# Selective scan in a vision tower: the input term made by TensorE from diagonals of B, decays in SBUF, the product with C split between GpSimd and VectorE

## What is computed

```python
xz = x_in @ W_in
x, z = (xz[..., :D], xz[..., D:])
proj = x @ W_x
B_ssm = proj[..., D:D + N]
C_ssm = proj[..., D + N:]
delta = jax.nn.softplus(delta_raw @ W_dt + b_dt)
A = -jnp.exp(A_log)
dA = jnp.exp(jnp.einsum('bld,dn->bldn', delta, A))
dBx = jnp.einsum('bld,bln->bldn', delta * x, B_ssm)
...
h = dA_t * h + dBx_t
y_t = jnp.einsum('bdn,bn->bd', h, C_t)
...
y = jnp.moveaxis(ys, 0, 1) + x * D_param
y = y * jax.nn.silu(z) @ W_out
```

## Time and profile before

| what | value |
| --- | --- |
| median of three runs | 780.34 us (776.89, 780.5, 780.34) |
| the profiled execution, its own time | 776.23 us |
| its span in the trace | 774.4 us |
| busy: PE, DVE, ACT, POOL | 689.5, 357.3, 255.4, 133.1 us |
| the first scan begins, the gated product begins | 203.87, 269.41 us |
| TensorE's mean granted clock | 0.989 |

### The profile page before, as it was taken

The page is one execution under the profiler, slowest core; times in us unless marked ns, Lnnn a source line. Parts: engine busy times, 40 slices in busy tenths (PEclk is TensorE's granted clock), DMA queues, the critical chain, the costliest instruction groups (busy, mean ns, idle before and its releaser), DMA issues.

```text
span 774.4 us, 16067 instructions
## 1 busy us (share of the span) xinstructions
PE 689.5 (89%) x6493; PEld 522.8 (68%) x6493; DVE 357.3 (46%) x1060; ACT 255.4 (33%) x639; POOL 133.1 (17%) x100
## 2 busy tenths in 40 slices
PE   9988879988866798989988989999977998999996
PEld 6665668875433356765754679888955556998985
DVE  3328640006999775667668641111136761111113
ACT  1332335543533414653691222222210122222221
POOL 2000200011399700131050220000040040000004
PEclk9999999999999999999999999999997999999999
DMA  8950179915566130000002789999228046899903
GB/s 310 405 217 0 36 240 422 375 62 197 156 150 149 36 123 1 0 1 0 1 0 83 306 279 353 348 378 348 98 64 349 1 176 214 345 357 363 363 29 92
DMA packets 30932, 143.85 MB, mean 186 GB/s; under 512 B 4624, under 2 KB 16720, under 8 KB 24336
## 3 DMA queue, kind: packets, MB, share of 16 engines
q1 hardware_dynamic: 23888, 132.86, 46.6%
q0 software_dynamic: 2240, 5.90, 2.4%
q10 hardware_dynamic: 4736, 4.13, 1.6%
HBM read 133.15 MB, written 9.71 MB: 184 GB/s over the span
## 4 chain that ended last, share of the span: by engine, by line
PE 55%; DVE 17%; issue 11%; DMA 6%; POOL 5%; ACT 3%; SPq 1%; DVEq 0%; POOLq 0%; ACTq 0%
PE PS L556 52%; DVE arena L2037 5%; POOL arena L1519 2%; DMA arena<-w_moe 2%; PE PS L615 1%; DMA x_slots<-XH,posu 1%; DMA arena<-y_slots,posu 1%; PE PS L579 1%; DVE stats L1600 1%; DVE stats L1593 1%; POOL arena L1545 1%; DMA arena<-bc_scratch 1%; DVE arena L2162 1%; DMA y_slots<-arena 1%; POOL arena L1532 1%
## 5 line engine op out<-in xcount | busy, mean ns | idle before, releaser
L556 PE MATMUL PS<-arena 128*64 128x64 f32 (+4 forms) x3132 | 243.9, 264 | 13.9 <-issue 5.2
L556 PEld LDWEIGHTS PS<-arena 128*64 128x64 f32 (+1 forms) x3132 | 203.8, 153 | 46.5 <-issue 20.8
L1823 DVE TENSOR_TENSOR arena<-arena,PS 128x384 f32<-128x384 f32 (+1 forms) x66 | 26.9, 407 | 183.4 <-ACT arena L1201 183.4
L556 PE MATMUL PS<-warm 128*128 128x512 bf16 (+2 forms) x425 | 97.5, 364 | 14.9 <-DVE rs L1584 13.5
L1519 POOL DMA_INDIRECT arena<-y_slots,posu x25 | 23.6, 945 | 312.2 <-DMA y_slots<-arena 305.5
L556 PEld LDWEIGHTS PS<-warm 128*128 128x128 bf16 (+1 forms) x425 | 38.7, 101 | 56.4 <-DVE rs L1584 16.8
L1201 ACT ACTIVATE arena<-PS 128x384 f32<-128x384 f32 (+1 forms) x66 | 27.2, 413 | 137.5 <-PE PS L556 137.5
L1532 POOL TENSOR_TENSOR arena<-arena 128x1152 f32<-128x1152 f32 x16 | 56.3, 3521 | 33.6 <-DVE arena L2037 33.6
L556 PE MATMUL PS<-arena,ident 128*128 128x512 f32 (+1 forms) x128 | 38.0, 440 | 21.5 <-POOL arena L1532 21.5
L556 PE MATMUL PS<-arena,wsh 128*128 128x128 f32 (+3 forms) x612 | 54.8, 260 | 1.3 <-ACT arena L1193 0.7
L556 PEld LDWEIGHTS PS<-arena,wsh 128*128 128x128 f32 (+1 forms) x612 | 48.6, 167 | 5.8 <-issue 2.8
(11 more groups left out here) (304 smaller groups left out, 929.7 us busy)
## 6 DMA issues: line engine op xcount, KB each, us to landing
arena<-w_moe SPq DMA_DIRECT2D x24, 2176.0 KB, 9.3
arena<-w_moe SPq DMA_DIRECT2D x9, 2052.0 KB, 10.8
wsh<-w_moe SPq DMA_DIRECT2D x8, 2176.0 KB, 9.9
arena<-bc_scratch SPq DMA_DIRECT2D x32, 288.0 KB, 3.9
wsh<-w_moe SPq DMA_DIRECT2D x3, 2052.0 KB, 12.0
y_slots<-arena ACTq DMA_DIRECT2D x19, 128.0 KB, 9.3
wx<-w_moe SPq DMA_DIRECT2D x1, 2176.0 KB, 17.6
wx<-w_sh SPq DMA_DIRECT2D x1, 2176.0 KB, 8.6
```

The lines of the kernel that those rows point to most:

```text
L556: return nc.tensor.matmul(out_, l, r, start=start, stop=stop, skip_group_check=True)
L1823: ins = v.tensor_tensor(firsts(hid_b[x][:, 0:full], n_), firsts(sg_s[x][:, 0:full], n_), firsts(PS[:, 2 * x + 1, 0:full], n_), ALU.mult)
```

## The change

TensorE now makes dBx. For each state and each tile of 128 tokens (the fifth has 64) ScalarE writes a diagonal matrix with the B values of that state's tokens (`state_diagonal`: the identity, scaled per partition by `BT`), and TensorE multiplies the transposed dx (`dxT`, tokens on partitions) with it: the product is dx with each token scaled, channels on partitions again, in PSUM (`XB`, one buffer per half). For that, TensorE computes B with tokens on partitions (ten products of 16 columns), and transposes dx (ten transposes, copied to SBUF by VectorE). The decays go to SBUF, two buffers per half (`dA`). VectorE's wide product is gone; the product with C is split along the tokens: GpSimd takes the first 480 of 576, VectorE the last 96, and in the last state 160 and 416. The loads of B rows are gone, and C rows are loaded once TensorE has read `hC` (hc_read). `keep_warm(3)` is removed.

```diff
-            return (PS[:, 0:2] if m else PS[:, 2:4])[:, :, 0:TH]
-        dA = [PS[:, 3 + 2 * d:5 + 2 * d, :].rearrange("p b c -> p (b c)")[:, 0:T] for d in range(KD)]
+            return (PS[:, 0:2] if m % 2 else PS[:, 2:4])[:, :, 0:TH]
+        XB = [PS[:, 4 + 2 * d:6 + 2 * d, :].rearrange("p b c -> p (b c)")[:, 0:T] for d in range(KD)]
-        dBx = part(8 * U1, 2, KD, T)
+        dA = part(8 * U1, 2, KD, T)
-        bcB = part(14 * U1, 4, T)
+        diagB = part(14 * U1, 2, NT, 128)
+        BT = part(14 * U1 + 2 * NT * 128, NT, NS)
+        C_CUT, C_CUT_LAST = 480, 160
...
-                    sp.wait_ge(sem("dbx_done"), 4 * i + (n - 3))
-                    sp.dma_start(bcB[:, n], bc_scratch[bass.ds(4 * i + n, 1), :].to_broadcast([128, T]))\
-                        .then_inc(sem(f"B{n}"), 16)
-                    sp.wait_ge(sem("hc_done"), 4 * i + (n - 1))
+                    sp.wait_ge(sem("hc_read"), 4 * i + (n - 1))
...
-                    pe.wait_ge(sem("xz_read"), m)
+                    pe.wait_ge(sem("xz_read"), m - 1)
                 from_xt([XZ_PS(m)[:, h, :] for h in range(2)], lambda k: win_s[:, k, 128 * m:128 * (m + 1)], "xz_psum")
+                if m == 1:
...
+                    for j in range(NT):
+                        for k in range(KD):
+                            last = mm(PS[:, 4, NS * j:NS * (j + 1)], XT[:, k, TT * j:TT * (j + 1)], wx_s[:, k, D:D + NS],
+                                      k == 0, k == KD - 1)
...
+            pe.wait_ge(sem("dx_ready"), 2)
+            for j in range(NT):
+                for d in range(KD):
+                    at = D * (j % 2) + 128 * d
+                    last = nc.tensor.transpose(PS[0:TILE_N[j], 5 + j // 2, at:at + 128], dx[:, d, tsl(j)], ident[:, :])
...
+            def state_input(n, d, p):
+                pe.wait_ge(sem("scan_half"), 2 * n + (d + 1))
+                for j in range(NT):
+                    last = mm(XB[d][:, tsl(j)], dxT[j][0:TILE_N[j], 128 * d:128 * (d + 1)], diagB[0:TILE_N[j], p, j, 0:TILE_N[j]])
+                last.then_inc(sem("xb"), 1)
+            def state_output(n, p):
+                pe.wait_ge(sem("hc_done"), n + 3)
+                pe.wait_ge(sem("hc_dve"), n + 1)
+                for d, ts, acc in Y_PARTS:
+                    last = mm(acc, ident[:, :], hC[:, p, d, ts], False, False)
+                last.then_inc(sem("hc_read"), 1)
...
-            keep_warm(3)
...
+            with pe.Fori(0, NS // 2 - 1) as i:
+                for p in range(2):
+                    pe.wait_ge(sem("diag_b"), 2 * i + (p + 4))
+                    for d in range(KD):
+                        state_input(2 * i + (p + 2), d, p)
+                    state_output(2 * i + p, p)
...
+                    last = nc.scalar.activation(diagB[0:n_, p, j, 0:n_], ident[0:n_, 0:n_], ACT.Copy, scale=BT[0:n_, j, bass.ds(n, 1)])
...
+                    act.wait_ge(sem("xb"), 4 * i + (2 * p + 2))
+                    state_diagonal(2 * i + (p + 2), p)
+                    for d in range(KD):
+                        act.wait_ge(sem("scan_half"), 4 * i + (2 * p + d + 3))
+                        decay(2 * i + (p + 2), d, p)
...
+                nc.gpsimd.tensor_tensor(hC[:, n % 2, :, 0:to], hs_[:, n % 2, :, 0:to],
+                                        bcC[:, n:n + 1, 0:to].to_broadcast([128, KD, to]), ALU.mult)\
+                    .then_inc(sem("hc_done"), 1)
...
-                v.tensor_tensor(dBx[:, n % 2, :, :], dx[:, :, :], bcB[:, n:n + 1, :].to_broadcast([128, KD, T]), ALU.mult)\
-                    .then_inc(sem("dbx_done"), 1)
...
+                    dve.wait_ge(sem("xb"), 8 * i + (2 * n + d + 1))
-                    v.tensor_tensor_scan(hs_[:, n % 2, d], dA[d], dBx[:, n % 2, d], 0.0, ALU.mult, ALU.add)\
+                    v.tensor_tensor_scan(hs_[:, n % 2, d], dA[:, n % 2, d], XB[d], 0.0, ALU.mult, ALU.add)\
...
+            def weigh(i, n, at):
+                dve.wait_ge(sem("scan_half"), 8 * i + (2 * n + 4))
+                dve.wait_ge(sem("hc_read"), 4 * i + (n + 1))
+                dve.wait_ge(sem(f"C{n}"), 16 * i + 16)
```

More of the change, by code:

```diff
@@ L938, in _ @@
             pe.sem_inc(sem("hc_read"), 2)
-            keep_warm(3)
[L940 to L945, removed]
+            state_input(1, 1, 1)
+            with pe.Fori(0, NS // 2 - 1) as i:
[4 more added lines that the diff above has]
+                    state_output(2 * i + p, p)
+            for p in range(2):
+                state_output(NS - 2 + p, p)
             idle_products(7)
@@ L1338, in _ @@
                 act.wait_ge(sem("dt_u"), m + 1)
-                nc.scalar.activation(dBx[:, 1, m], dBx[:, 0, m], ACT.Ln).then_inc(sem("dt_ln"), 1)
+                nc.scalar.activation(dA[:, 1, m], dA[:, 0, m], ACT.Ln).then_inc(sem("dt_ln"), 1)
                 xz_copy(m)
-            act.wait_ge(sem("A_ready"), 1)
[L1342 to L1350, removed]
@@ L1352, in _, with state_diagonal @@
-            decays(0)
+            act.wait_ge(sem("dxt_psum"), 1)
+            nc.scalar.activation(BT[:, :, :], PS[:, 4, 0:NT * NS].rearrange("p (j n) -> p j n", n=NS), ACT.Copy)\
+                .then_inc(sem("diag_b"), 1)
+            act.wait_ge(sem("diag_b"), 1)
+            def state_diagonal(n, p):
+                for j in range(NT):
+                    n_ = TILE_N[j]
+                    last = nc.scalar.activation(diagB[0:n_, p, j, 0:n_], ident[0:n_, 0:n_], ACT.Copy, scale=BT[0:n_, j, bass.ds(n, 1)])
+                last.then_inc(sem("diag_b"), 1)
@@ L1353, in _, with decay @@
+            def decay(n, d, p):
+                nc.scalar.activation(inner(dA[:, p, d]), inner(dl[:, d, :]), ACT.Exp, scale=A_s[:, d, bass.ds(n, 1)])\
+                    .then_inc(sem("dA_ready"), 1)
+            state_diagonal(0, 0)
+            act.wait_ge(sem("A_ready"), 1)
+            act.wait_ge(sem("delta_ready"), KD + 1)
+            for d in range(KD):
+                decay(0, d, 0)
             for m in range(KD, 2 * KD):
                 xz_copy(m)
-            with act.Fori(1, NS) as n:
-                decays(n)
+            state_diagonal(1, 1)
@@ L1357, in _ @@
+            for d in range(KD):
+                decay(1, d, 1)
+            with act.Fori(0, NS // 2 - 1) as i:
+                for p in range(2):
+                    act.wait_ge(sem("xb"), 4 * i + (2 * p + 2))
+                    state_diagonal(2 * i + (p + 2), p)
+                    for d in range(KD):
+                        act.wait_ge(sem("scan_half"), 4 * i + (2 * p + d + 3))
+                        decay(2 * i + (p + 2), d, p)
             nc.scalar.activation(zs[:, :, :], zs[:, :, :], ACT.Silu).then_inc(sem("z_silu"), 1)
@@ L2032, in scan @@
+            for q, (j, n) in enumerate(PAIRS):
+                dve.wait_ge(sem("dxt_psum"), q + 2)
+                for i in range(j, j + n):
+                    ins = v.tensor_copy(dxT[i][0:TILE_N[i], :], PS[0:TILE_N[i], 5 + q, D * (i - j):D * (i - j + 1)])
+                    if i < j + n - 1:
+                        mark(ins)
+                    else:
+                        ins.then_inc(sem("dx_ready"), 1)
             def scan(i, n):
-                dve.wait_ge(sem("dbx_done"), 4 * i + (n + 1))
```

53 lines of the change are left out of this document (28 added, 25 removed).

## The result

| | before | after |
|---|---|---|
| median of four runs | 780.42 us (776.89 to 780.58) | **799.57 us** (798.83 to 801.07) |
| ratio | | 1.0263, 95% interval 1.0231 to 1.0294 |
| profiled execution's own time | 776.23 | 799.39 |
| its span | 774.4 | 797.3 |
| granted clock of TensorE | 0.989 | 0.985 |

The account below looks back on a forecast made before the run. TensorE was to bound the scan loop at 4.42 us a state; with a 3.7 us later start, the sum was +10.8 us: 787.0 on the profiled 776.23, 791.1 on the median 780.34. Forecast 789.0 in between, range 779 to 803.

Parts of the forecast that it names:

- The bound and the direction: In the scan loop, TensorE was to become the bound at 4.42 us a state against 3.92 before, making the kernel slower.
- One sign: In the scan loop, VectorE was to stand idle about 1.3 us a state, with TensorE as releaser.
- So I take 0.115 for all 20, the 64-column ones too: 1.15 a half, 2.30 a state: TensorE's twenty thin input instructions per state were to go at a pitch of 0.115 us each, 2.30 us a state.
- The term 4.42: TensorE's time per state in the scan loop: 2.30 us for input products plus 2.12 for output products.
- The start: At the head of the stage, the first scan was to come 3.7 us later, at 207.5 instead of 203.87.
- The sum of 787.0: Whole kernel: the gated product 10.8 us later, at 280.2 instead of 269.41, added to the profiled execution's 776.23 us.
- Rival 1: In the scan loop, VectorE keeps setting the round, thin TensorE instructions at half the pitch: -6 us, 774; chance 0.08.
- rival 2: Whole kernel about unchanged, the thin instructions' pitch near the turning point of 0.078 us: 777 to 784, 781; chance 0.09.
- Rival 3: In products with C, GpSimd starts first and blocks VectorE in every state: 22.9 us, with the start +26.6, 806; chance 0.07.
- if VectorE's small product lasts over 1 us: Sign in the scan loop that the forecast is wrong and Rival 3 holds; the product was forecast at 0.36 us.
- Rival 4: In the scan loop, ScalarE or the thin products' sequencing sets about 4.9 us a state: +8 more, 797; chance 0.08.
- Hand-offs and loads: In the scan loop, hand-offs were to fit in 4.42 us, TensorE never waiting, and row loads to cost nothing.

Follow-up runs that it names:

- padded: The kernel after, with the fifth token tile's input product contracting over 128 rows instead of 64, the added rows zeros: 792.74 us, ratio 1.0191 to the kernel before.
- reordered: The kernel after, with the 64-row tile's product issued first instead of last in the second half of the channels: 797.97 us, ratio 1.025 to the kernel before.
- merged: The kernel after, with a state's two 64-column output products made into one of 128 columns: 798.99 us, ratio 1.026 to the kernel before.
- half-and-half kernel: Against the kernel before: VectorE makes dx times B for channel half 0, TensorE for half 1, with some smaller edits; 774.51 us, ratio 0.9927.

## Why the prediction was right and wrong

- **The bound and the direction: right.** TensorE has no idle time in the loop, the clock there is full, ScalarE, VectorE and GpSimd wait for it. A state costs what TensorE's products cost, in the kernel after and in the padded, reordered and merged versions of it. One sign came true by luck: VectorE is idle 1.3 us a state, as told, but of a round of 5.06 and not of 4.42, since its own work is 3.7 and not 3.1.
- **The step that failed: "So I take 0.115 for all 20, the 64-column ones too: 1.15 a half, 2.30 a state".** The 0.115 itself was good: without turns the twenty take 2.23 (0.1115 each), in the padded run. But the rows it was taken from the earlier trace rows were streams over 128 rows alone, and the prediction looked at the fifth tile's 64 columns and not at its 64 contraction rows: the turns stand in the sum at nothing, without a reason. This stream changes its number of contraction rows four times a state, and each change costs 0.17: 2.85 instead of 2.30 for the inputs, and 2.21 instead of 2.12 for the outputs. The term 4.42 measured 5.06; the padded run measured 4.39. Sixteen states at 0.55 and seventeen output groups at 0.09 would be 10.3 us, and the stretch from first scan to gated product missed the sum by 82.1 - 72.7 = 9.4.
- **The start: right.** 3.7 forecast, 3.8 measured. The input projections, the transposes and the copies came in the order told. Two small misses offset each other: the copies were faster (1.74 for five instead of 2.1), and the first input half, with its turn, took 1.56 to the scan (208.98 to 210.54) instead of 1.3.
- **Ahead of the stage: nothing in the sum.** The sum of 787.0 stood on the profiled 776.23, the faster of two executions of the same kernel that were profiled. With 9.4 for the turns and 2.9 for the part ahead it reaches 799.3, and the profiled run took 799.39; the 2.9 are read from that run itself, so this only says that nothing else is missing. The later stages are unchanged, as forecast, to 0.4 us.
- **The middle of two bases.** The stage's sum is +10.8 us, yet 789.0 is only 8.7 above the median of 780.34, because it is halfway between a sum on the profiled execution and one on the median. A difference has to be added to the same kind of number that it is compared with: 780.34 + 10.8 + 9.4 is 800.5, beside a median of 799.57.
- **Rival 1, VectorE keeps setting the round, and rival 2, no change:** refuted. Both needed a pitch of about 0.08 us or less; it is 0.1115. The 81 ns of the Trainium skill (TensorE: Matmul & The Clock Gate, "Back-to-back issue gap") do not hold for these f32 instructions of 128 columns, while the columns / 1.2 GHz of its section "LDWEIGHTS (loading the stationary operand)", an estimated 107 ns, come near. That section has a load over fewer rows cost the same as one over 128; this stream shows that the turn between the two has a price of its own, 0.17 us.
- **Rival 3, GpSimd first and VectorE stands still:** the mechanism is there, in every other state: GpSimd starts at 232.71 and VectorE's 192 elements at 232.75, and they take 2.40 instead of 0.36. The Trainium skill (SBUF — State Buffer, "Who interferes with whom") says that a VectorE instruction with two SBUF inputs and a GpSimd instruction that reads SBUF contend, and that the order of issue decides who is held; the trace agrees, since VectorE's product ends 0.2 us after GpSimd's. So the sign "if VectorE's small product lasts over 1 us" was met. Its price is nil here: the rival's 22.9 us needed it in every state, it came in every other one, where scans and product are 2.40 + 2.59 = 4.99 of TensorE's 5.06, and the kernel without the split has the same round.
- **Rival 4, some 4.9 a state, 797:** nearest in numbers, and it named the place, the sequence of the thin products, but not the cause. Its ground was dispatches with registers: the padded run keeps them all and has 4.39. ScalarE is busy for 42.1 of 74.25 us and waits for TensorE (2.23 us before its diagonals).
- **Hand-offs and loads:** no wait of TensorE in the loop, and none for rows of B or C.

## What to carry to other kernels

Count a stream of small products by the turns in it as well as by their number: a short tail tile padded with zeros to the full 128 rows cost nothing and gave back 0.67 us a state, and where it can't be padded, its products are put side by side. Before work is moved from a full engine to another, add up the other's state with the work on it; here 4.4 against 3.9 said that all of it was too much, and half of it (some 3.2 a state on TensorE and as much on VectorE), with some smaller edits, turned +2.6% into -0.7%. And take the sum on more than one profile of the kernel before, or on stretches cut at fixed landmarks: two profiles of one kernel differed by 3.8 us of span, none of it in the stage under change. Two counts that go together, such as time at half clock and a late start, are not yet a cause: following the rows put the delay elsewhere.

## What the runs showed of the hardware

- A change between contractions over 128 rows and over 64 rows in a stream of f32 products costs 0.16 to 0.17 us each time (5.06, 4.74 and 4.39 us a state with four, two and no turns). Why was not tried further; that the next weights can't be loaded ahead across the turn is only a guess.
- Between them, f32 products of 128 and of 64 columns with new weights each go at the same 0.1115 us an instruction on average (2.23 us for twenty in the padded run).
- A VectorE product of SBUF inputs of 192 elements takes 0.36 us alone and 2.40 when it starts 0.04 us after a GpSimd product of 960, whose own 2.22 isn't lengthened. Scans with one source in PSUM beside GpSimd keep their 1.35 (233.85 in the half-and-half kernel, beside GpSimd's product from 233.36).
- Stretches of TensorE at 1.2 GHz come and go from one execution to the next in parts of the program that no edit touches, 3.6 or 6.8 us of them near 110 us in two profiles of the same kernel, and so do waits for transfers (0.56 or 2.47 us, 0.85 or 2.23 us at the same instructions). A stage measured between its own landmarks repeats to 0.01 us (82.00 and 81.99); the whole time doesn't.
